# Longer iterations in the first convolution of a graph kernel: 12 gathered and 10 bucketed groups with 12 orderings, and an earlier load of the places

## The chip, the cores and the metric

The kernel runs on 1 core of one Trainium2 chip. The metric is the device time of one execution in microseconds (us), as the median of several runs; lower is better.

## The reference

The function works on a graph of 12500 nodes with 32 features each and 200000 edges, whose destinations are sorted and whose sources are random. It first applies a layer normalisation and an equivariant message-passing layer (a small network per edge, products with spherical harmonics, a sum over the edges at each destination). Then, after another normalisation, it applies three graph convolutions, of 32 to 128, 128 to 128 and 128 to 32 features:

```
h = x @ W
msg = h[src] * norm[:, None]
out = segment_sum(msg, dst) + b      # self loops are among the edges
```

with a rectifier after each. The change concerns only the first of the three convolutions (n = 1 in the code). There the kernel sums the rows of a normalised table (96 bf16 numbers per node: three bf16 parts of 32 features) over the edges, before it multiplies by W1.

## The kernel before

**Two ways to fetch a source's row.** In each convolution the edges are divided. "Gathered" groups of 1024 edges fetch the rows of their sources from DRAM: SyncE loads the 1024 indices (L556), GpSimd issues 8 indirect DMAs of 128 rows (L676), and TensorE sums the 8 tiles into a window of 128 destinations with a one-hot matrix (`gathered_sum`, L1860); VectorE adds the window to the accumulator `accT` (L1532) and makes the next group's one-hot matrix (L1434). Four row buffers rotate, so GpSimd may start group g only when group g-4 has been added. "Bucketed" groups of 1408 edges never touch the table in DRAM: their edges were ordered by the block of 128 nodes that holds the source, and one-hot matrices on both sides, made on the chip, pick and sum the rows of a table that lies in SBUF.

**Chunks.** A bucketed group is worked off in NCK = 5 chunks. For each chunk ScalarE makes the source matrix for the chunk that follows, in two instructions (`near_sources` L845, `mark_sources` L854), and copies out what TensorE took (`copy_bucket` L867); TensorE takes 20 small products (`take`, L1790) and gives 5 (`give`, L1804); VectorE makes the destination matrix (L1419). All these are double buffered, by chunk, with each wait on the chunk two before. The source matrices need the group's "places", an 800 KB load that spreads one row of DRAM over 128 partitions (`load_places`, L828, issued by ScalarE). It has two buffers, by the parity of the group.

**Ordering.** The places are themselves computed in the first convolution, for all 96 bucketed groups of the kernel: 2 before it starts, 94 during it. One ordering ("rank") takes three chunks: VectorE compares (`count_blocks`, L1322 first) when k % 3 is 0, TensorE counts (L1765), ScalarE copies the counts (`copy_prefix`, L836) when k % 3 is 1, VectorE ranks (`rank_edges`, L1337 to L1359), TensorE spreads (`place_values`, L1772 and L1774) and VectorE keeps the result (`keep_places`, L1365 to L1372) when k % 3 is 0 again, just ahead of the next `count_blocks`. ScalarE stores it to DRAM (`store_places`, L818) when k % 3 is 2. Of the ranks of an iteration the first OWN are for this convolution's own groups, the others for groups that only the later convolutions take.

**The loop.** `sweep` writes the first and the last iteration out, with constants, and runs those between in a hardware loop. `LOOP[n]` and `REST[n]` say how many gathered and bucketed groups an iteration and the last one have. Before the change they are (8, 6) and (12, 16) for n = 1: 10 iterations of 30 chunks with 8 ranks each (9 of them in the loop), and a last one of 80 chunks with 14 ranks. In an iteration the ranks fill chunks 0 to 23, and chunks 24 to 29 have none; in the last they fill chunks 0 to 41, and 42 to 79 have none. Gathered groups start at evenly spread chunks (`shape`).

**The load's place.** The load of the next group's places is issued in a group's third chunk (c == 2), after that chunk's `copy_bucket`, and after its `copy_prefix` if it has one. It waits until the store of those places has landed. The places are first read in the body of the group's last chunk (c == 4), where ScalarE runs `near_sources` for the next group's first chunk.

Of the kernel before, what the change touches and what calls it, by code (L numbers as in the profile page):

```python
# [38 lines left out]
UNROLL = 4  # L39
# [16 lines left out]


GATHERED = [NG, 92, 100, 64]
LOOP = [(UNROLL, 0), (8, 6), (12, 8), (8, 12)]
REST = [(UNROLL, 0), (12, 16), (16, 14), (8, 12)]  # L60
ITS = [NIT] + [(GATHERED[n] - REST[n][0]) // LOOP[n][0] + 1 for n in (1, 2, 3)]
E0 = GATHERED[3] * GE
BJ = 11
# [12 lines left out]
BIAS = F3  # L76
KC = 5

RANKS = 8
OWN = LOOP[1][1]  # L80
SLOTS = 2
RANKING = 13
NCK = KB // KC
# [8 lines left out]
OWN_LAST = BUCKETED[1] - 2 - OWN * (ITS[1] - 1)  # L92
RANKS_LAST = OWN_LAST + OTHERS - (RANKS - OWN) * (ITS[1] - 1)
assert RANKS % SLOTS == 0 and 3 * RANKS <= LOOP[1][1] * NCK and OWN_LAST == REST[1][1] - 2
assert OWN_LAST <= RANKS_LAST and 3 * RANKS_LAST < REST[1][1] * NCK


NORM0 = sqrt(4 * pi) / sqrt(2 * MUL)
# [21 lines left out]
def gnn_kernel(nc, x, src, dst, edge_attr, edge_weight, w1, b1, w2, b2,  # L120
               W1, B1, W2, B2, W3, B3, out):
    ctx = ExitStack()
    with ctx:
# [575 lines left out]
        def _(act):  # L699
# [170 lines left out]
            def conv(n):  # L870

                def body(step, first, last):
                    groups, chunks_, starts_at = shape(n, last)
                    u = -1
                    for k in range(chunks_):
                        if k in starts_at:
                            u, at = u + 1, k
                            held = (starts_at + [chunks_])[u + 1] - k
                            ahead = n == 2 and not (last and u == groups - 1)
                        more = not (last and k == chunks_ - 1)  # L880
                        if n == 1 and more:
                            near_sources(step, k + 1)
                        if ahead and k == at:
                            onehot_waits(n, step, u + 1, first)
                            distances(step, u + 1, range(TPG // 2))
                        if ahead and k == min(at + 1, at + held - 1):
                            distances(step, u + 1, range(TPG // 2, TPG)).then_inc(dist_ready[(u + 1) % 2], 1)
                        if ahead and k == min(at + 2, at + held - 1):
                            onehot_of_distances(n, step, u + 1)
                        if n == 1 and more:  # L890
                            mark_sources(step, k + 1)
                        copy_bucket(n, step, k)
                        v, c = divmod(k, NCK)
                        if n == 1 and k % 3 == 1 and k // 3 < (RANKS_LAST if last else RANKS):
                            copy_prefix(step, k // 3)
                        i = (k - 2) // 3 - 1
                        if n == 1 and k % 3 == 2 and 0 <= i < (RANKS_LAST if last else RANKS):
                            store_places(step, i, last)
                        if n == 1 and c == 2 and not (last and k + NCK >= chunks_):
                            load_places(n, step, v + 1)  # L900
                        if n > 1 and c == NCK - 1 and not (last and k + 2 * NCK >= chunks_):
                            load_places(n, step, v + 2)

                if n == 1:
                    near_sources(Step(act, 0, n), 0)
                    mark_sources(Step(act, 0, n), 0)
                if n == 2:
                    make_onehot(n, Step(act, 0, n), 0, True)
                sweep(act, body, n)

            def first_places(n):
# [46 lines left out]
        def _(dve):  # L958
# [538 lines left out]
            def conv(n):  # L1497
                rows_ = WIDTH[n]

                def ranking(step, k, last):  # L1500

                    i, part = divmod(k, 3)
                    most = RANKS_LAST if last else RANKS
                    if part == 0:
                        if 0 < i <= most:
                            keep_places(step, i - 1, last)
                        if i < most:
                            count_blocks(step, i, last)
                    elif part == 1 and i < most:
                        rank_edges(step, i, last)  # L1510

                def body(step, first, last):
                    groups, chunks_, starts_at = shape(n, last)
                    u = -1
                    for k in range(chunks_):
                        more = not (last and k == chunks_ - 1)
                        if more and n > 1:
                            mark_sources(n, step, k + 1)
                        mark_destinations(n, step, k)
                        if k in starts_at:  # L1520
                            u += 1
                            if u % UNROLL == 0:
                                start = load_registers(starts, step, u, N - 1)
                                n_far = load_registers(further, step, u, NB)
                            far_windows(n, step, u, n_far[u % UNROLL])
                            dve.wait_ge(*when(group_summed, step, u, before=convs_before(n)))
                            dve.wait_ge(*when(added, step, u - 1, before=rounds_before(n)))
                            v_done = (k - 7) // NCK
                            if not no_chunk(n, step, v_done * NCK):
                                dve.wait_ge(bucket_added, bucket_count(n, step, v_done))  # L1530
                            window = bass.ds(start[u % UNROLL], WIN)
                            v.tensor_tensor(accT[0:rows_, window], accT[0:rows_, window], sums[0:rows_, u % 2, 0:WIN],  # L1532
                                            ALU.add).then_inc(added[u % UNROLL], 1)
                            if n != 2:
                                if not (last and u == groups - 1):
                                    make_onehot(n, step, u + 1, first)
                                if not (last and u >= groups - 2):
                                    pair_numbers(n, step, u + 2)
                        if k % NCK == 1 and not (first and k == 1):
                            add_bucket(n, step, (k - 1) // NCK - 1, u)  # L1540
                        if n != 2 and k % NCK == NCK - 2 and not (last and k + 2 >= chunks_):
                            pair_destinations(n, step, k // NCK + 1)
                        if n == 1:
                            ranking(step, k, last)
                    if last:
                        add_bucket(n, step, chunks_ // NCK - 1, groups - 1)
                if n == 1:
                    dve.reg_mov(far_count, 0)
                if n != 2:
                    begin = Step(dve, 0, n)  # L1550
                    v.tensor_copy(iota_ps.bitcast(fp32), iota_h[:, :].bitcast(fp32))
                    v.tensor_copy(iota1_ps.bitcast(fp32), iota1_h[:, :].bitcast(fp32)).then_inc(iota_set, 1)
                    for u in range(2):
                        pair_numbers(n, begin, u)
                    pair_destinations(n, begin, 0)
                    dve.wait_ge(iota_set, 1 if n == 1 else 2)
                    make_onehot(n, begin, 0, True)
                if n > 1:
                    mark_sources(n, Step(dve, 0, n), 0)
                sweep(dve, body, n)  # L1560
                dve.wait_ge(bucket_added, sum(BUCKETED[:n + 1]))
                if n == 1:
                    v.tensor_reduce(odd_i[:, NBG:NBG + 1], odd_i[:, 0:NBG], X, ALU.max).then_inc(odd_counted, 1)
                    dve.wait_ge(odd_counted, 1)
                odd_edges(n)
                v.memset(flag[:, :], 0.0).then_inc(conv_done, 1)
# [63 lines left out]
        def _(pe):  # L1630
# [219 lines left out]
            def conv(n):  # L1850
# [14 lines left out]
                def body(step, first, last):  # L1865
                    groups, chunks_, starts_at = shape(n, last)
# [17 lines left out]
                                    place_values(step, i)  # L1884
                    if last:
                        give(n, step, chunks_ - 1)
                if n == 1:
                    pe.reg_mov(far_count, 0)
                    pe.wait_ge(acc_set, NCH)
                    for i in (-2, -1):  # L1890
                        count_prefix(Step(pe, 0, 1), i)
                        place_values(Step(pe, 0, 1), i)
# [86 lines left out]
```

## Time and profile before

| | before |
|---|---|
| median of 3 runs | 5388.06 us (5382.95 to 5391.85) |
| the profiled execution | 5381.47 us, its span 5379.6 us |
| busy over the span | PE 85%, PEld 60%, DVE 74%, ACT 58%, POOL 66% |
| mean granted TensorE clock | 0.85 of full speed |

The profile is one execution, followed instruction by instruction. PE is TensorE's matmuls, PEld its weight loads, DVE VectorE, ACT ScalarE, POOL GpSimd, SP SyncE; a "q" behind the name is that engine's issue of DMAs. A line number is that of the kernel above. A bracket behind an instruction says how long its engine had been idle before it, and what released it. The first convolution's first VectorE rank of the swept part is at 2365 us, its last instruction on the accumulator at 3450 us: some 1090 us of 5380.

### The profile page before, as it was taken

How to read it: one execution, taken by the hardware profiler on the slowest of the kernel's cores; microseconds unless marked ns; L12 is line 12 of the kernel's file. 1: busy time of each engine (PE TensorE's matmuls, PEld its weight loads, DVE VectorE, ACT ScalarE, POOL GpSimd, SP SyncE). 2: the span in 40 equal slices, each digit the busy share in tenths (PEclk: the TensorE clock that was granted, in tenths of full speed). 3: DMA queues.
4: the chain of work that ended last, by engine and by line, in shares of the span. 5: the costliest groups of instructions: out<-in, count | busy, mean ns of one | idle time of the engine just before them, and what ended most of it. 6: DMA issues, size and time to landing. Idle time of an engine off the chain costs nothing. (4 is left out here: it accounts for less than half of the span.)

```text
span 5379.6 us, 146653 instructions
## 1 busy us (share of the span) xinstructions
PE 4570.9 (85%) x51651; PEld 3244.5 (60%) x51652; DVE 3990.6 (74%) x9508; ACT 3122.0 (58%) x6228; POOL 3551.7 (66%) x3635
## 2 busy tenths in 40 slices
PE   2999999999999999946666666699999999877777
PEld 1555555555555555534555455588888899655656
DVE  5999999999999999977777777344444444366665
ACT  2666666666666666457777777655555554344442
POOL 3777777777777777457777774177777774177774
PEclk9999999999999999955555555699999999577676
DMA  6111111111111111232222222333333332344443
GB/s 73 37 36 36 36 36 38 36 36 36 36 38 36 36 36 36 34 64 76 76 77 76 83 76 70 112 104 110 104 110 104 110 106 80 98 143 146 139 152 99
DMA packets 464109, 398.70 MB, mean 74 GB/s; under 512 B 252172, under 2 KB 437360, under 8 KB 462948
## 3 DMA queue, kind: packets, MB, share of 16 engines
q10 hardware_dynamic: 143252, 205.78, 11.1%
q0 software_dynamic: 115712, 109.02, 9.4%
q1 hardware_dynamic: 204496, 75.06, 6.6%
q8 instruction: 430, 7.05, 0.5%
q14 instruction: 219, 1.79, 0.1%
HBM read 374.23 MB, written 15.28 MB: 72 GB/s over the span
## 5 line engine op out<-in xcount | busy, mean ns | idle before, releaser
L676 POOL DMA_INDIRECT rows<-table,idx x3616 | 3536.0, 978 | 1768.8 <-issue 1097.2
L733 ACT ACTIVATE dist<-iota,rel 128x128 f32<-128x128 f32 x2368 | 735.3, 391 | 840.0 <-PE sums L1684 804.9
L1684 PE MATMUL sums<-scratch,onehot 128*128 128x393 f32 x3136 | 1122.2, 500 | 50.9 <-DVE scratch L1176 47.0
L1673 PE MATMUL radial<-w2n,shared 65*128 65x384 f32 x3136 | 1081.3, 488 | 98.4 <-ACT shared L756 98.4
L1790 PE MATMUL radial<-arena,shared 128*32 128x96 bf16 (+1 forms) x31200 | 917.9, 264 | 272.8 <-ACT shared L854 182.7
L1684 PEld LDWEIGHTS sums<-scratch,onehot 128*128 128x128 f32 x3136 | 579.6, 190 | 553.8 <-issue 97.0
L1790 PEld LDWEIGHTS radial<-arena,shared 128*32 128x32 bf16 (+1 forms) x31200 | 654.3, 114 | 401.7 <-ACT shared L854 192.2
L1673 PEld LDWEIGHTS radial<-w2n,shared 65*128 65x128 f32 x3136 | 581.4, 190 | 512.0 <-ACT shared L756 98.0
L1152 DVE TENSOR_TENSOR scratch<-radial,shared 128x768 f32<-128x768 f32 x784 | 737.6, 941 | 0.0
L867 ACT CAST scratch<-radial 128x480 bf16<-128x480 f32 x860 | 473.5, 551 | 402.7 <-PE radial L1790 387.3
L1804 PE MATMUL psT<-shared,scratch 128*96 128x96 bf16 (+1 forms) x3900 | 475.9, 271 | 108.1 <-DVE shared L1419 97.6
L1804 PE MATMUL psX<-shared,scratch 128*96 128x96 bf16 (+1 forms) x3900 | 473.6, 271 | 79.0 <-DVE shared L1419 74.4
L1144 DVE TENSOR_TENSOR scratch<-radial,shared 128x512 f32<-128x512 f32 x784 | 529.7, 676 | 8.3 <-PE radial L1673 3.0
L1390 DVE TENSOR_SCALAR shared<-scratch,line 128x640 bf16<-128x640 bf16 (+1 forms) x830 | 396.6, 478 | 164.4 <-PE radial L1790 95.4
L1804 PEld LDWEIGHTS psT<-shared,scratch 128*96 128x96 bf16 (+1 forms) x3900 | 392.9, 179 | 188.8 <-DVE shared L1419 85.8
L1804 PEld LDWEIGHTS psX<-shared,scratch 128*96 128x96 bf16 (+1 forms) x3900 | 396.5, 180 | 150.1 <-DVE shared L1419 83.5
L1162 DVE TENSOR_REDUCE scratch<-scratch 128x64 f32<-128x1024 f32 x392 | 471.2, 1202 | 0.0
L756 ACT ACTIVATE shared<-shared,b1c,w1c 64x1024 f32<-64x1024 f32 x196 | 439.4, 2242 | 0.4 <-DVE relX L1064 0.4
L1532 DVE TENSOR_TENSOR accT<-accT,sums 96x128 f32 (+1 forms) x256 | 73.0, 285 | 488.7 <-PE sums L1860 473.9
L1860 PE MATMUL sums<-onehot,rows 128*128 128x128 f32 (+1 forms) x2848 | 361.2, 289 | 83.5 <-DMA rows<-table,idx 72.7
L863 ACT COPY scratch<-radial 128x384 f32<-128x384 f32 x350 | 167.4, 478 | 440.8 <-PE radial L1790 419.9
L1419 DVE TENSOR_TENSOR shared<-radial,shared 128x480 bf16<-128x480 bf16 x860 | 338.4, 399 | 107.0 <-PE psX L1804 37.9
(180 smaller groups left out, 4709.0 us busy)
## 6 DMA issues: line engine op xcount, KB each, us to landing
scratch<-places_d ACTq DMA_DIRECT2D x242, 800.0 KB
rows<-table,idx POOLq DMA_INDIRECT x3616
shared<-in_edge_weight SPq DMA_DIRECT2D x195, 256.0 KB, 3.5
idx<-in_src SPq DMA_DIRECT2D x451, 4.0 KB
arena<-norm_d ACTq DMA_DIRECT2D x4, 1568.0 KB, 12.3
table<-arena SPq DMA_DIRECT2D x24, 256.0 KB, 2.4
table<-arena SPq DMA_DIRECT2D x2, 1176.0 KB, 10.6
table<-arena SPq DMA_DIRECT2D x24, 96.0 KB, 2.0
```

Source lines behind the costliest of these rows:

```text
L676: (pool.indirect_dma_start(rows_3[:, r, j, :] if n in (1, 3) else rows[:, r, j, 0:WIDTH[n]], None, tables[n], bass.IndirectOffsetOnAxis(ap ...
L733: ins = nc.scalar.activation(dist[:, j, :], iota[:, :], ACT.Abs, scale=-1.0, bias=rel[:, bass.ds(step.tile(u) + j, 1)])
L756: nc.scalar.activation(hidT[0:HID0, u % 2, 0:tiles, 0:used], ew_row[:, u % 2, 0:tiles * used].rearrange("c (p j) -> c j p", j=tiles), ACT. ...
L867: nc.scalar.copy(taken[n][:, h, :, :], radial[0][:, h, 0:KC * F3].rearrange("p (t f) -> p t f", f=F3)).then_inc(bucket_copied, 1)
L1144: prod = v.tensor_tensor(prodA[:, h, t:t + 2, :].rearrange("p t (m s) -> p t m s", s=16), R[:, :, 0:256].rearrange("p t (m s) -> p t m s", ...
L1152: last = v.tensor_tensor(msg[:, h, t:t + 2, 17:401].rearrange("p t (i u s) -> p t i (u s)", i=3, u=MUL), R[:, :, 256:384].unsqueeze(2).to_ ...
L1162: v.tensor_reduce(msg[:, h, :, 0:16], prodA[:, h, :, :].rearrange("p t (m s) -> p t m s", s=16), X, ALU.add).then_inc(scalars_ready[h], 1)
L1390: v.tensor_scalar(from_src[n][:, k % 2, :, :, :], places[v_ % 2][:, :, c * KC * CAP:(c + 1) * KC * CAP].rearrange("p i (t r) -> p i t r", ...
L1673: last = nc.tensor.matmul(radial[q % 2][:, k, 0:RDIM], hidT[:, u % 2, 2 * q + k, :], w2n[:, :], start=True, stop=True)
L1684: last = nc.tensor.matmul(sums[:, u % 2, 0:SEGW], onehot[:, u % 2, 4 * h + k, :], msg[:, h, k, MUL:MUL + SEGW], start=(h == 0 and k == 0), ...
L1790: last = nc.tensor.matmul(d, from_src[n][:, h, i, t, :], table_of(n, s), start=True, stop=True, tile_position=(0, 32 * i))
L1804: last = nc.tensor.matmul((psX if v % 2 else psT)[0:w, 0:BWIN], taken[n][:, h, t, :], to_dst[n][:, h, t, :], start=(c + t == 0), stop=(c * ...
```

## The change

The first convolution's iterations become longer: LOOP (12, 10) and REST (8, 6), with 12 ranks in each. ITS[1] falls from 11 to 8: 7 iterations of 50 chunks (6 of them in the loop) and a last one of 30. The groups of each kind stay 92 and 76, the ranks 94. In an iteration the ranks now fill chunks 0 to 35 and chunks 36 to 49 have none; the last iteration has 10 ranks, which fill all of its 30 chunks, and the end of the tenth is written out behind the chunks. The next group's places are loaded in a group's second chunk instead of its third.

```
-LOOP = [(UNROLL, 0), (8, 6), (12, 8), (8, 12)]
-REST = [(UNROLL, 0), (12, 16), (16, 14), (8, 12)]
+LOOP = [(UNROLL, 0), (12, 10), (12, 8), (8, 12)]
+REST = [(UNROLL, 0), (8, 6), (16, 14), (8, 12)]
...
-RANKS = 8
+RANKS = 12
...
-assert OWN_LAST <= RANKS_LAST and 3 * RANKS_LAST < REST[1][1] * NCK
+assert OWN_LAST <= RANKS_LAST and 3 * RANKS_LAST == REST[1][1] * NCK
...
-                        if n == 1 and c == 2 and not (last and k + NCK >= chunks_):
+                        if n == 1 and c == 1 and not (last and k + NCK >= chunks_):
                             load_places(n, step, v + 1)
...
+                    if last and n == 1:
+                        store_places(step, RANKS_LAST - 1, last)
...
+                    if last and n == 1:
+                        keep_places(step, RANKS_LAST - 1, last)
                     if last:
                         add_bucket(n, step, chunks_ // NCK - 1, groups - 1)
...
                     if last:
                         give(n, step, chunks_ - 1)
+                    if last and n == 1:
+                        place_values(step, RANKS_LAST - 1)
```

## Rows read from the trace of the kernel before

**Rows 1.** Busy time by stage: a looped iteration, then chunks of the last without ranks.
```profile
core 0: us, PE busy (x) PEld busy (x) DVE busy (x) ACT busy (x) POOL busy (x), PEclk, DMA share, GB/s
2542.30:2630.30 88.00, 54.95 (x989) 44.71 (x993) 64.55 (x224) 62.29 (x97) 62.86 (x65) 0.52 0.29 78
3363.50:3433.30 69.80, 39.04 (x800) 29.82 (x800) 19.84 (x67) 60.74 (x91) 12.35 (x14) 0.51 0.24 77
```
**Rows 2.** Waits in the first convolution, 2355.8 to 3450.2 us: total, times, longest.
```profile
ACT arena L836 <- PE radial L1765: 127.3, 73, 2.8
ACT shared L845 <- DMA scratch<-places_d: 125.6, 64, 9.8
POOL rows L676 <- DVE accT L1532: 111.6, 46, 11.8
...
DVE arena L1337 <- ACT arena L836: 32.8, 50, 2.7
```
**Rows 3.** L1322 on VectorE, one instruction for each rank: count, first and last start.
```profile
L1322 DVE TENSOR_TENSOR arena<-radial,arena x94: 871/892/893, 2365.0 to 3357.1; 128x1408 bf16<-128x1408 bf16 x94
```
**Rows 4.** Timeline of L1322 on VectorE: a looped iteration, and the last's first rank.
```profile
3068.80 0.88 DVE L1322 TENSOR_TENSOR arena<-radial,arena 128x1408 bf16<-128x1408 bf16 x1
...
3077.68 0.89 DVE L1322 TENSOR_TENSOR arena<-radial,arena 128x1408 bf16<-128x1408 bf16 x1
...
3086.67 0.89 DVE L1322 TENSOR_TENSOR arena<-radial,arena 128x1408 bf16<-128x1408 bf16 x1
...
3095.45 0.89 DVE L1322 TENSOR_TENSOR arena<-radial,arena 128x1408 bf16<-128x1408 bf16 x1
...
3132.12 0.89 DVE L1322 TENSOR_TENSOR arena<-radial,arena 128x1408 bf16<-128x1408 bf16 x1
...
3157.73 0.88 DVE L1322 TENSOR_TENSOR arena<-radial,arena 128x1408 bf16<-128x1408 bf16 x1
...
3244.55 0.88 DVE L1322 TENSOR_TENSOR arena<-radial,arena 128x1408 bf16<-128x1408 bf16 x1
```
**Rows 5.** Timeline of ScalarE after an iteration's last rank: loads, waits and free chunks.
```profile
3134.54 0.41 ACTq L828 DMA_DIRECT2D scratch<-places_d  x1
...
3138.75 0.83 ACT L845 ACTIVATE shared<-scratch,line 128x640 bf16<-128x640 bf16 x1 [1.62 <-DMA scratch<-places_d]
...
3140.78 0.83 ACT L845 ACTIVATE shared<-scratch,line 128x640 bf16<-128x640 bf16 x1
...
3145.91 0.41 ACTq L828 DMA_DIRECT2D scratch<-places_d  x1
...
3150.77 0.83 ACT L845 ACTIVATE shared<-scratch,line 128x640 bf16<-128x640 bf16 x1 [1.75 <-DMA scratch<-places_d]
```
**Rows 6.** Timeline at the loop's return: TensorE's last and next take; VectorE's first instruction.
```profile
3148.62 0.59 PE L1790 MATMUL radial<-arena,shared 128*32 128x96 bf16 x20 [0.87 <-ACT shared L854]
...
3151.56 0.41 DVE L1419 TENSOR_TENSOR shared<-radial,shared 128x480 bf16<-128x480 bf16 x1 [3.37 <-issue]
...
3154.56 0.59 PE L1790 MATMUL radial<-arena,shared 128*32 128x96 bf16 x20 [4.78 <-ACT shared L854]
```
**Rows 7.** Waits from 3360 to 3450 us, the last iteration's chunks without ranks.
```profile
ACT shared L845 <- DMA scratch<-places_d: 8.8, 7, 2.9
```
**Rows 8.** Timeline of VectorE: one rank from its first to its last instruction; the convolution's end.
```profile
2547.62 0.89 DVE L1322 TENSOR_TENSOR arena<-radial,arena 128x1408 bf16<-128x1408 bf16 x1
...
2556.43 0.18 DVE L1372 CAST shared<-arena 128x32 f32 x1
...
3449.94 0.25 DVE L1494 TENSOR_TENSOR accT<-accT,psX 96x96 f32 x1 [3.14 <-PE psX L1804]
```
**Rows 9.** Timeline of ScalarE: a store in chunk 5, `copy_bucket` of chunk 6, `copy_prefix` in 7.
```profile
2463.37 0.38 ACTq L818 DMA_DIRECT2D places_d<-src_at  x1
...
2465.93 0.54 ACT L867 CAST scratch<-radial 128x480 bf16<-128x480 f32 x1
...
2470.98 0.27 ACT L836 CAST arena<-radial 128x128 bf16<-128x128 f32 x1 [1.87 <-PE radial L1765]
```
**Rows 10.** Writes to DRAM: KB each, us from issue to landing.
```profile
table<-arena SPq DMA_DIRECT2D x24, 96.0 KB, 2.0
...
bucket_start_d<-arena SPq DMA_DIRECT2D x1, 0.4 KB, 7.3
```
**Rows 11.** Instruction fetches of the iteration from 2542.3 to 2630.3 us: packets, MB, share.
```profile
q8 instruction: 11, 0.18, 0.9%
```
**Rows 12.** GpSimd's gathers in the same iteration: busy, mean ns, idle before them.
```profile
L676 POOL DMA_INDIRECT rows<-table,idx x65 | 63.8, 981 | 25.4 <-issue 20.2 <-DVE accT L1532 5.3
```

## Prediction

> **What bounds the kernel now.** Only the first convolution changes, so I read that stretch, 2356 to 3450 us. The table by stages comes first [rows 1]: in a looped iteration of 88.0 us VectorE is busy 64.6, ScalarE 62.3 and GpSimd 62.9 us, so no engine is full; where no ranks run, ScalarE is busy 60.7 of 69.8 us, and it sets the pace. Then the waits [rows 2]: GpSimd waits 111.6 us for VectorE's adds. It is ahead of the others by its four buffers, so the gathers don't bound. ScalarE waits 127.3 us for a rank's counts and 125.6 us for places. The question is which of these waits lie on the path.
>
> The starts of L1322, one per rank, give the rhythm [rows 3, 4]. From the first to the eighth rank of an iteration it is 3132.12 - 3068.80 = 63.3 us, 9.05 per rank of three chunks. From the eighth to the next iteration's first it is 25.6 us, for nine chunks of which six have no rank. Ten iterations take 3244.55 - 2365.0 = 879.6 us, so the mean gap from a last rank to the next first is 87.96 - 7 x 9.05 = 24.6 us. The last iteration's 13 intervals take 3357.1 - 3244.55 = 112.6 us, and from its last rank to the final add it is 3450.2 - 3357.1 = 93.1 us [rows 3, 4, 8]. So the convolution is 83 intervals (633.5 + 112.6 = 746.1 us), ten gaps (246) and a tail (93.1): 1085 us.
>
> In a chunk without a rank ScalarE needs 3140.78 - 3138.75 = 2.03 us, unless it waits for places: 1.62 us in chunk 24 and 1.75 us in chunk 29 [rows 5]. Each return of the loop costs more: TensorE's take of the next iteration comes 3154.56 - 3148.62 = 5.94 us after the last one where 2.03 is the rhythm, 3.9 us lost, and VectorE had nothing to run for 3.37 us [rows 6]. The wait of chunk 29 lies inside this: the source matrix was ready at 3150.77 + 1.69 = 3152.5 us, TensorE began 2.1 us later. (The 1.69 is two instructions of 0.83 and the step between them.)
>
> **The change part by part.** Chunks (380), gathers, ranks (94) and ranks in written-out code (22) keep their numbers.
>
> *Intervals.* They grow from 83 to 86 (7 x 11 + 9): +3 x 9.05 = **+27.2 us**.
>
> *Gaps.* They fall from ten to seven, and each gets 8 more chunks without a rank at 2.03: 24.6 + 16.3 - 1.6 = 39.3 us. The 1.6 is chunk 24's wait for places, which the earlier load ends (below). 7 x 39.3 = 275 against 246: **+29 us**. Three returns of the loop less, 11.7 us, are in this.
>
> *Tail.* It had 38 chunks without a rank. Now the tenth rank ends the iteration: from L1322 to its last kept value a rank takes 2556.43 + 0.18 - 2547.62 = 9.0 us [rows 8]. TensorE's last give stands ahead of the values (0.6 us, the take of 20 being the nearest row of its size [rows 6]), and the value read and final add stand behind (I take 0.9, of which the add is 0.25): 10.5 us. 93.1 to 10.5: **-82.6 us**. Nothing hides these 10.5 us. The last store and the load for the second convolution come later by this much too; that load is covered by the tables made between the convolutions, and uncovered it would cost its landing, under 5 us.
>
> *The load one chunk earlier.* Its issue is followed by the landing after 3138.75 - 3134.54 = 4.2 and 3150.77 - 3145.91 = 4.9 us. ScalarE was free 1.75 us before the second landing, 3.1 us after the issue; one more chunk makes this 5.1 us, so the wait goes. In the gaps and the tail it is counted above. Among ranks ScalarE has slack: it waits for the counts anyway. There I compare two intervals with one gathered group each, the second (3077.68 to 3086.67, 8.99 us) with a wait for places and the third (8.78) without [rows 4]: 0.21 us per load, and three of five loads wait in this way, some 35 in all: **-7.4 us**. The bounds of this term are 0 (ScalarE's slack hides all) and the whole wait: 125.6, less 8.8 in the last iteration's tail [rows 2, 7] and about 10 x (1.6 + 1.75) in the gaps, is 83 us. I take the value near 0 because it is the one measured on intervals. At the seven returns that remain the load's wait is worth nothing, since TensorE is later; at most 7 x 1.75 = 12 us.
>
> *A store just ahead of a load.* The places of an iteration's third group are stored in chunk 5 and were loaded in chunk 7; now they are loaded in chunk 6, some 3.0 us behind the store (2463.37 to 2465.93 + 0.44) [rows 9]. No row shows when such a store has landed. The nearest writes to DRAM took 2.0 and 7.3 us [rows 10]. With 2.0 nothing waits. With 7.3 ScalarE waits 4.3 us with the next `near_sources` queued behind, of which 1.87 us were idle before the counts [rows 9]: 2.4 x 8 = +19 us. I take 0, since the 7.3 us was a write of 4 bytes per descriptor. The Trainium skill (DMA: Bandwidth & Descriptors, Anatomy of one DMA) puts a DMA's fixed cost at about 2.0 us and adds that a write to HBM can take surprisingly long; by its 2.0 the sum would be the same, by its warning nearer to +19.
>
> *Gathers.* A group costs GpSimd 8 x (0.98 + 0.31) = 10.3 us [rows 12], the 0.31 being 20.2 us of issue over 65. Twelve take 124 us of an iteration that I put at 11 x 9.05 + 39.3 = 139 us, so its lead stays.
>
> **Sum.** 27.2 + 29 - 82.6 - 7.4 = -34 us, from 5381.5 us of the profiled execution to 5347.5. This execution was 6.6 us below the median of the runs; from the median the forecast is **5354 us**. The layout alone would give little: with waits for places at 1.3 to 1.8 us left in the gaps (42.2 us each) it is 27.2 + 49.3 - 82.6 = -6 us. The load's place is most of the gain.
>
> **Rivals.** *The rank's chain runs through ScalarE's wait as well.* For it: ScalarE reads the counts right after it catches up, and VectorE waits 32.8 us for that copy [rows 2]. Against: the interval pair above. If half to all of the 83 us came back, 5388 - 34 - (34 to 76) = 5278 to 5320.
>
> *The wait for places stays.* The load lands later because it meets other transfers, or the gain is taken up by a later wait. For it: landings differ by 0.7 us between two neighbours and the longest wait is 9.8 us [rows 2, 5]. Against: the margin of 5.1 us covers both. It would leave the layout's -6: 5382.
>
> *The store is late*, as above: -34 + 19, 5373.
>
> *Slower: the longer body is not fetched in time.* An iteration fetches 11 packets of instructions for 30 chunks [rows 11], so the whole body is fetched anew each time; 50 chunks make 18, about 130 in seven iterations. The one place where a fetch shows is the loop's return, 3.4 us of idle VectorE [rows 6]. If one packet in five were waited for at that price, it is 26 x 3.4 = +88 us, and 5442; the sign turns at 10 packets (34 us). Against it: inside an iteration no engine shows such a stall now, over 10 x 11 packets. The Trainium skill (Runtime: NRT & Kernel Launch, Instruction fetch mechanics) says that the fetch of sequential blocks is mostly hidden and a taken branch out of the window stalls; by it this rival gives 0 and the three returns saved stand.
>
> **How the numbers follow.** Forecast 0.66, its own range 5335 to 5375; rank chain 0.13; waits stay 0.12; late store 0.04; slower 0.05. The range of 8 in 10 goes from 5308, inside the first rival, to 5383, past the second. What a measurement can tell from no change is about 0.2%, 10.8 us. Faster takes the forecast, the first rival and the late store, 0.83; within 0.2% the waits that stay, 0.12; slower 0.05.
>
> **What would show it.** Right: the wait of L845 for places falls from 125.6 to below 20 us; free chunks at 2.03 us throughout; L1322 intervals near 9.0 us, seven gaps near 39 us, and about 10 us from the last L1322 to the final add; GpSimd still waiting for L1532. Wrong: a gap above 42 us; a wait of ScalarE for a store of places in chunk 6; intervals of 8.5 us or less, which would mean the first rival; idle "issue" time of TensorE or VectorE inside an iteration, which would mean the last.

## The result, and the profile after

The kernel after takes **5365.11 us** (median of 5 runs, 5359.89 to 5372.49), the kernel before on the same chip 5387.14 us (5 runs, 5379.18 to 5391.85). The ratio is 0.9962, with an interval of 0.9951 to 0.9973: about 20 us faster. The profiled execution of the kernel after took 5365.11 us with a span of 5363.1; the one of before took 5381.5 us, with a span of 5379.6. So the two traces differ by 16.5 us, less than the medians do.

The forecast was 5354 us, inside a range of 5308 to 5383. The total falls in it, but that hides two things which nearly undo each other: the first convolution gained as much as was forecast, and the second, which the change doesn't touch, lost half of it again. The rows that show it are the end marks of the convolutions, a MEMSET of `flag` at the end of each. In the kernel before:

```profile
3451.40 0.06 DVE L1566 MEMSET flag<- 128x1 f32 x1 [0.93 <-DVE odd_i L1563]
...
4579.80 0.06 DVE L1566 MEMSET flag<- 128x1 f32 x1 [0.91 <-DVE accT L1494]
...
5333.30 0.06 DVE L1566 MEMSET flag<- 128x1 f32 x1 [1.25 <-issue]
```

In the kernel after, the same timeline of VectorE:

```profile
3417.31 0.06 DVE L1570 MEMSET flag<- 128x1 f32 x1 [1.24 <-issue]
...
4562.74 0.06 DVE L1570 MEMSET flag<- 128x1 f32 x1 [0.92 <-DVE accT L1496]
...
5316.86 0.06 DVE L1570 MEMSET flag<- 128x1 f32 x1 [0.91 <-DVE accT L1496]
```

The first convolution ends 3451.40 - 3417.31 = 34.1 us sooner. The second takes 4562.74 - 3417.31 = 1145.4 us where it took 1128.4: **17.0 us more**. The third takes 754.1 against 753.5. The sum, -34.1 + 17.0 + 0.6 = -16.5, is the difference of the spans.

**The first convolution after.** L1324 is the rank's first instruction, which was L1322. Its count and its first and last start (to [rows 3]), then the table by stages for one looped iteration (to [rows 1]):

```profile
L1324 DVE TENSOR_TENSOR arena<-radial,arena x94: 872/891/892, 2365.1 to 3406.4; 128x1408 bf16<-128x1408 bf16 x94
```

```profile
core 0: us, PE busy (x) PEld busy (x) DVE busy (x) ACT busy (x) POOL busy (x), PEclk, DMA share, GB/s
2774.42:2913.44 139.02, 90.02 (x1641) 72.49 (x1644) 101.04 (x348) 104.91 (x163) 94.82 (x96) 0.52 0.32 80
```

An iteration of 50 chunks takes 139.02 us, as the prediction put it (139). The shares are near those of [rows 1]: VectorE 0.73 in both, ScalarE 0.75 against 0.71, GpSimd 0.68 against 0.71. The timeline of L1324 shows where an iteration's ranks end and the next one's begin (to [rows 4]):

```profile
2774.42 0.88 DVE L1324 TENSOR_TENSOR arena<-radial,arena 128x1408 bf16<-128x1408 bf16 x1
...
2873.15 0.89 DVE L1324 TENSOR_TENSOR arena<-radial,arena 128x1408 bf16<-128x1408 bf16 x1
...
2913.44 0.88 DVE L1324 TENSOR_TENSOR arena<-radial,arena 128x1408 bf16<-128x1408 bf16 x1
```

From the first to the twelfth rank it is 98.73 us, 8.98 per interval, and the gap to the next iteration is 40.3 us. The waits of the first convolution, 2355.8 to 3417 us (total, times, longest; to [rows 2]):

```profile
ACT arena L836 <- PE radial L1769: 173.8, 94, 2.7
...
POOL rows L676 <- DVE accT L1534: 102.4, 44, 4.3
...
ACT shared L845 <- DMA scratch<-places_d: 15.1, 13, 9.6
```

ScalarE's wait for places fell from 125.6 to 15.1 us, and its wait for a rank's counts rose from 127.3 to 173.8. That is the slack among ranks: ScalarE comes earlier to a wait that was there before. A store in chunk 5 and the load that depends on it in chunk 6, on ScalarE (to [rows 9]):

```profile
2786.82 0.37 ACTq L818 DMA_DIRECT2D places_d<-src_at  x1
...
2787.78 0.83 ACT L845 ACTIVATE shared<-scratch,line 128x640 bf16<-128x640 bf16 x1
2788.85 0.38 ACTq L828 DMA_DIRECT2D scratch<-places_d  x1
...
2789.82 0.83 ACT L845 ACTIVATE shared<-scratch,line 128x640 bf16<-128x640 bf16 x1
```

The load goes out 2.03 us behind the store, and the next L845 comes 2.04 us after the last: nothing waited. At the loop's return (the jump back to the start of its body) the first instruction of TensorE and of ScalarE in the next iteration (to [rows 6]):

```profile
2910.26 0.59 PE L1794 MATMUL radial<-arena,shared 128*32 128x96 bf16 x20 [3.44 <-issue]
...
2910.24 0.83 ACT L845 ACTIVATE shared<-scratch,line 128x640 bf16<-128x640 bf16 x1 [2.16 <-issue]
```

And the end, from the last rank's kept value to the final add (to [rows 8]); the last L1324 starts at 3406.4:

```profile
3414.75 0.16 DVE L1374 CAST shared<-arena 128x32 uint8<-128x32 f32 x1
3415.55 0.25 DVE L1496 TENSOR_TENSOR accT<-accT,psX 96x96 f32 x1 [0.64 <-issue]
```

The tail is 3417.31 - 3406.4 = 10.9 us to the mark, where before it was 94.3 to the mark.

**The second convolution after.** TensorE is its bound: from 3417 to 4562 us it is busy 1113.78 of 1145 us. The rows list each fp32 product of the kernel as two matmuls, so the 20 products of a take are x40. TensorE's timeline at returns of this convolution's loop:

```profile
3839.18 0.73 PE L1794 MATMUL radial<-arena,shared 128*32 128x128 f32 x17 [2.02 <-DVE shared L1392]
3842.97 1.51 PE L1794 MATMUL radial<-arena,shared 128*32 128x128 f32 x23 [3.07 <-issue]
...
4098.38 0.73 PE L1794 MATMUL radial<-arena,shared 128*32 128x128 f32 x17 [2.42 <-issue]
4101.69 1.50 PE L1794 MATMUL radial<-arena,shared 128*32 128x128 f32 x23 [2.58 <-issue]
```

The take of 40 matmuls is cut after the 17th, and TensorE stands still with nothing that the profile shows it to wait for. The convolution has eight iterations, of which the first and the last are written out and six are run by the loop, so the loop returns five times. All five returns show this cut, with idle times of 1.70, 3.07, 2.79, 2.58 and 2.58 us; the step into the loop and the step out of it show none. The kernel before has one gap at a return, ahead of the take, and none inside or behind it:

```profile
4122.72 2.26 PE L1790 MATMUL radial<-arena,shared 128*32 128x128 f32 x40 [2.40 <-issue]
4124.91 2.69 PE L1860 MATMUL sums<-onehot,rows 128*128 128x128 f32 x16
```

The table by windows says the same. Before, then after, one stretch of 250 us of the second convolution (TensorE's busy time is the first number behind the length):

```profile
3750.00:4000.00 250.00, 245.41 (x4376) 221.26 (x4376) 109.23 (x200) 142.20 (x376) 189.98 (x198) 0.99 0.35 108
```

```profile
3750.00:4000.00 250.00, 240.02 (x4245) 216.22 (x4240) 106.10 (x194) 136.58 (x361) 189.02 (x197) 0.97 0.36 104
```

5.4 us of 250 are lost here, with two returns in it; VectorE and ScalarE do less in the same time because they wait for TensorE.

The gaps are not all of the loss. Over the second convolution TensorE is idle for 31.6 us where it was 18.9, 12.8 more, and busy for 1113.8 us where it was 1109.6, 4.2 more for the same 19394 matmuls. The clock has a part in this. Ten us from the start of the first take behind a return, before and then after:

```profile
4122.72:4132.72 10.00, 10.00 (x159) 9.03 (x160) 3.69 (x8) 5.11 (x14) 7.71 (x8) 0.83 0.28 77
```

```profile
4098.38:4108.38 10.00, 7.42 (x90) 6.58 (x94) 0.94 (x3) 3.19 (x10) 4.06 (x5) 0.66 0.23 61
```

A granted clock of 0.83 is 3.4 us of the 10 at the 1.2 GHz level, and 0.66 is 6.8 us. It comes behind the idle time at the return. In the kernel before it is 3.4 us long at four of the five returns and absent at one; in the kernel after it is 6.8 us at all five, and so it is in the four other versions with the loss. The 16 matmuls behind the take then need 3.61 us at this return, where the kernel before needs 2.69. So the clock adds to what the gaps cost.

**The theories.** What has to be settled is which part of the change gained the 34 us, and what lost the 17. For the loss, theory A: the new loop body shifted TensorE's instruction stream behind it, so that the target of the second loop's return now lies just ahead of the boundary of a block that is fetched as one, and the block behind it comes too late. An iteration's fetches support a block of this kind, 16.4 KB per packet:

```profile
q8 instruction: 16, 0.26, 0.8%
```

Theory B: something else that the layout leaves behind when the second convolution starts (the late last store, the load behind it, the state of the buffers). Theory C: the load's place.

### The profile page after: what moved, and what is told of

Read it like the earlier page. It is cut to its first block, busy times and chain, and to the rows that moved or that the text cites. A ratio compares the mean times of both kernels' runs of the same rounds, so it can differ in the third digit from the quotient of the medians.

```text
span 5363.1 us, 146734 instructions
## 1 busy us (share of the span) xinstructions
PE 4561.7 (85%) x51651; PEld 3237.4 (60%) x51652; DVE 3982.0 (74%) x9508; ACT 3120.8 (58%) x6228; POOL 3548.8 (66%) x3635
## 4 chain that ended last, share of the span: by engine, by line
PE 27%; POOL 9%; issue 8%; DVE 8%; ACT 2%; DVEq 1%; DMA 1%; ACTq 0%; POOLq 0%; SPq 0%
POOL rows L676 9%; PE radial L1794 8%; PE psT L1808 5%; PE psX L1808 4%; PE sums L1864 4%; PE radial L1769 2%; ACT shared L845 1%; DVE arena L1324 1%; DVE arena L1347 1%; PE radial L1925 1%; DVE arena L1343 1%; PE radial L1961 1%; PE radial L1776 1%; PE sums L1933 1%; ACT scratch L867 1%
## 5 line engine op out<-in xcount | busy, mean ns | idle before, releaser
L1864 PEld LDWEIGHTS sums<-onehot,rows 128*128 128x128 f32 (+1 forms) x2848 | 318.5, 190 | 133.5 <-DMA rows<-table,idx 69.6
```

The lines of the kernel that those rows point to most:

```text
L1864: mm = nc.tensor.matmul(sums[0:w, u % 2, 0:WIN], far_rows[j], (onehot if n == 2 else onehot_3)[0:used, u % 2, j, :], start=(j == 0), stop= ...
```

## Experiments

**One part alone.** The first kernel is after with the load back at a group's third chunk, the second is before with the load at the second.

```diff
-                        if n == 1 and c == 1 and not (last and k + NCK >= chunks_):
+                        if n == 1 and c == 2 and not (last and k + NCK >= chunks_):
```

> The changed kernel with the load of the places back in a group's third chunk. From the prediction: in the first convolution -6 us against before (that is 28 us more than the changed kernel has), with L845 waiting some 100 us or more for places again. Theory A (the 17 us that the second convolution lost come from where its loop lies in TensorE's instruction stream): this kernel's stream on TensorE is that of the changed one, so the second convolution takes 1145 us as in the changed kernel, and the whole is -6 + 17 = +11 us against before. Theory B (they come from the earlier load or from what it moves in DRAM): the second convolution is back at 1128 us and the whole is -6.

Measured: 5402.93 us against 5385.64, ratio 1.0037 (1.0024 to 1.0051): **slower than before**, by 17 us where +11 was expected. Its first convolution ends at 3454.47 us, 3.1 behind before, and ScalarE waits 130.9 us for places. Its second takes 1148.6 us and has the same cut:

```profile
4138.48 0.73 PE L1794 MATMUL radial<-arena,shared 128*32 128x128 f32 x17 [2.65 <-issue]
4142.06 1.51 PE L1794 MATMUL radial<-arena,shared 128*32 128x128 f32 x23 [2.85 <-issue]
```

```diff
-                        if n == 1 and c == 2 and not (last and k + NCK >= chunks_):
+                        if n == 1 and c == 1 and not (last and k + NCK >= chunks_):
```

> The kernel before with the load of the places one chunk earlier and nothing else. From the prediction's terms: 16 us of waits in chunk 24 of ten iterations, 9 us in the last iteration's chunks without ranks, 7 us among the ranks: -32 us in the first convolution (range -25 to -60). Theory A: TensorE's stream is that of before, so the second convolution stays at 1128 us and the whole is -32 us. Theory B: the second convolution loses up to 17 us here, and the whole is -15.

Measured: 5340.58 us, ratio 0.9915 (0.9902 to 0.9929): some 25 us better than the whole change. That is 45 us faster than the kernel before, where 32 was expected. The first convolution ends at 3415.92 us in a profile that took 5346.2 us, 5.6 above this median: 35.5 sooner than in before. The second takes 1127.2. So the load's place is the gain, and the loss comes with the layout: theory C falls. On the first convolution the layout brought nothing: +3.1 us with the late load, and 3417.31 - 3415.92 = +1.4 with the early one, both within the scatter of single profiles (below).

**The stream shifted, the layout kept.** Both kernels put unneeded matmuls ahead of the second convolution in TensorE's stream: 16 in the kernel after, 30 in the kernel before. What they do is move everything that follows in the stream.

```diff
                 if n == 2:
+                    for i in range(16):
+                        nc.tensor.matmul(psT[0:1, 500:501], one[:, :], one[:, :], start=True, stop=True)
                     pe.wait_ge(acc_set, 2 * NCH)
```

> The changed kernel with 16 tiny matmuls (64 instructions of TensorE) between the first and the second convolution, in an unused corner of a PSUM bank. Theory A: the target of the second convolution's loop no longer lies some 36 instructions ahead of a 16 KB boundary, nor the third's some 14 ahead; the second gap inside the first take (17 of 40 matmuls, 2.6 to 3.1 us idle, 23 more) goes from every return; the second convolution falls from 1145 to about 1128 us, and the whole to -33 us against before. Theory B (data, buffers or the other engines' streams): the second convolution stays at 1145 us or gains under 4 us.

Measured: 5351.94 us, ratio 0.9936 (0.9923 to 0.995). More work, and 13 us faster than the kernel after. The cut is gone, the second convolution takes 1127.4 us, and TensorE is as busy as in before:

```profile
3750.00:4000.00 250.00, 245.06 (x4336) 221.40 (x4337) 107.84 (x199) 140.54 (x374) 190.29 (x197) 0.99 0.37 108
```

> The kernel before with 30 tiny matmuls (120 instructions of TensorE) at the same place, which puts both later loops at the place in the stream that they have in the changed kernel, within one instruction. Nothing else changes. Theory A: the second convolution rises from 1128 to about 1145 us with the take of 40 split 17 and 23 at each return, and the whole is +17 us against before. Theory B: no change beyond 3 us for the 30 matmuls.

Measured: 5405.93 us, ratio 1.0035 (1.0022 to 1.0049), the second convolution 1146.5 us. The old layout with the old load has the loss too once the stream behind it is shifted, and the cut now falls after the 13th matmul, where the 17th was expected:

```profile
4007.63 0.63 PE L1790 MATMUL radial<-arena,shared 128*32 128x128 f32 x13 [2.10 <-DVE shared L1390]
4010.93 1.92 PE L1790 MATMUL radial<-arena,shared 128*32 128x128 f32 x27 [2.67 <-issue]
```

Theory B falls with these two: the same layout with and without the loss, and the loss without the layout. The ten profiles at a mean granted clock of 0.85, those of the runs below included, fall into two groups in the second convolution: 1127.2 to 1128.8 us where no take is cut or followed by a gap, 1144.1 to 1148.6 where one is.

**How the loss grows with the place.** A first attempt: the same edit with 16 and 24 matmuls in the kernel before, and in a third kernel each group's places loaded yet a chunk earlier:

> The kernel before with 16 tiny matmuls (64 instructions of TensorE) at the same place as in the other padded kernels. The second convolution's loop target then lies about 93 instructions ahead of a 16 KB boundary of TensorE's stream (157 in the kernel before, 36 in the changed one), the third's about 70. Theory A (a second fetch is waited for only as far as the instructions between the target and the boundary don't cover it, about 0.02 to 0.03 us each in a take of fp32): the second gap is shorter by 57 instructions than in the changed kernel, 1 to 2 us instead of 2.8, and the second convolution takes 1132 to 1140 us. If the padding itself cost anything, it would show here as well: under 2 us. Rival (any crossing near the target costs the whole 17 us): 1145 us.

> The same with 24 tiny matmuls (96 instructions): the target about 61 instructions ahead of the boundary. Theory A: a gap between that of the 64-instruction kernel and the changed kernel's, 1138 to 1144 us in the second convolution. Rival: 1145 us, or 1128 where only very few instructions ahead of the boundary hurt.

```diff
-                        if n == 1 and c == 2 and not (last and k + NCK >= chunks_):
+                        if n == 1 and c == (1 if v == 1 else 0) and not (last and k + NCK >= chunks_):
```

> The kernel before with the places loaded in a group's first chunk (in the second group of an iteration in its second chunk, because that group's places are stored in its first). Against the kernel with the load alone in the second chunk, which waited 19.6 us for places of which 9.9 us once at the start: the remaining waits go, of which most lie where TensorE is later anyway. -35 to -42 us in the first convolution against before, 0 to -5 against that kernel; if ScalarE instead waits for the store of the same group's places (stored one to two chunks earlier), up to 3 us per iteration come back and it is slower than that kernel.

Measured: 8076.35, 8097.0 and 8064.88 us, with ratios of 1.0006 (0.9985 to 1.0027), 1.0021 (1.0002 to 1.004) and 0.9991 (0.9971 to 1.0011). On this chip every kernel took about 8,070 us at that time, before too (8072.4), with a mean granted clock of 0.73 where the other profiles have 0.85. Effects of a few microseconds don't stand out there, and the three answer nothing. They were run again:

> The kernel before with 16 unneeded matmuls (64 instructions of TensorE's stream) between the first and the second convolution. Stream-place theory with a graded cost: the second convolution's return target now lies some 93 instructions ahead of a 16 KB boundary (157 before, 36 in the kernel after), and TensorE crosses it only after the second packet has come, so the second convolution takes 1128 to 1140 us against 1128.4 before. Theory that any 16 added matmuls cost it something of the size seen with 30: 1137 us or more. The first convolution is unchanged in either case (flag at 3451 us).

Measured: 5404.06 us, ratio 1.0035 (1.0021 to 1.0048), the second convolution 1144.1 us. This is the whole loss, where theory A as I had put it, with a cost that grows with the place, allowed 1140 at most. The size was missed; the place was not. The gap now stands between the take of 40 and the next take of 16:

```profile
4008.62 1.68 PE L1790 MATMUL radial<-arena,shared 128*32 128x128 f32 x40 [2.98 <-issue]
4012.57 3.77 PE L1860 MATMUL sums<-onehot,rows 128*128 128x128 f32 x16 [2.27 <-issue]
```

> The same with 24 unneeded matmuls (96 instructions): the target lies some 61 instructions ahead of the boundary. Stream-place theory: the first take of 40 matmuls after a return is cut or nearly cut, and the second convolution takes 1136 to 1146 us, between the kernel before (1128.4) and 30 such matmuls (1146.5). A theory in which the place does nothing and only their number counts: 64 and 96 instructions lie on a line from 0 to the +18 us of 120, so +9.6 and +14.4 us.

Measured: 5401.04 us, ratio 1.0031 (1.0019 to 1.0043), the second convolution 1147.8 us, 1.8 above my range. The count theory wanted +9.6 and +14.4 us for the two, and they have +15.7 and +19.4, with +18.1 for 30 matmuls: no line through zero. The cut is after the 25th:

```profile
4006.65 0.95 PE L1790 MATMUL radial<-arena,shared 128*32 128x128 f32 x25 [2.37 <-issue]
4009.95 1.08 PE L1790 MATMUL radial<-arena,shared 128*32 128x128 f32 x15 [2.36 <-issue]
```

From 30 to 24 unneeded matmuls the cut moves from 13 to 25, two matmuls of the take for each one taken out. With eight fewer again it should be at 25 + 16 = 41, just behind the take of 40, which is where the kernel with 16 has it. For the kernel after, 16 unneeded ones move the cut from 17 to -15, that is, ahead of the target, and no return meets it. One rule fits these places. It isn't known why 30 unneeded matmuls, which were to put the loop where it stands in the kernel after, put the cut four matmuls sooner (13 for 17). The gap at the cut is 1.2 to 3.2 us over the 25 returns of the five kernels. The boundary itself is in no view; what the traces show is that the gap moves with the length of the stream, by the length added.

That leaves the question why the kernel before, whose boundary lies some 73 matmuls of this kind behind the target, doesn't pay. From the start of the first take to the first matmul behind the cut it is 3842.97 - 3839.18 = 3.8 us in the kernel after, 3.3 with 24 and 30, and 3.95 with 16 in the rows above, and 3.0 to 3.95 over all 25 returns, whatever stands ahead of the cut. So it looks like a race: TensorE can go past the boundary 3.0 to 4.0 us after the return has been served, and it loses what it reaches the boundary too early by. The trace's packets of queue q8 agree. At each of the 50 returns of the ten profiles one packet starts 0.4 to 1.3 us behind the start of the take and is done 1.5 to 2.3 us behind it, with or without a loss; where there is a cut, TensorE goes on 1.2 to 1.8 us after the packet. The trace doesn't say which engine a packet is for. A kernel between 0 and 16 tests this:

> The kernel before with 8 unneeded matmuls (32 instructions): the second convolution's return target lies some 125 instructions ahead of the boundary, between the kernel before (157, no second gap) and 16 such matmuls (93, a second gap and 1144 us). If TensorE and the fetch race each other, TensorE reaches the boundary about 1.3 us (40 matmuls) and two thirds of the next take of 16 (2 to 3.8 us) after the return, which is about the 3.3 to 4.0 us that the next packet took, so the gap is under 1 us and the second convolution takes 1128 to 1134 us. If what counts is only that unneeded matmuls stand there, it takes 1140 us or more, as with 16, 24 and 30.

Measured: 5390.22 us, ratio 1.0007 (0.9998 to 1.0016), the second convolution 1128.8 us, and no gap behind the take:

```profile
4003.32 2.36 PE L1790 MATMUL radial<-arena,shared 128*32 128x128 f32 x40 [3.71 <-issue]
4005.61 3.77 PE L1860 MATMUL sums<-onehot,rows 128*128 128x128 f32 x16
```

By the same rule the boundary is 25 + 32 = 57 of the take's matmuls behind the target: 40 are the take, the 16 behind it have the same two instructions each in the trace (one load of weights, one matmul), and a few waits stand between. That puts it at the end of the 16. The quickest of the five returns shows it there:

```profile
4256.77 1.30 PE L1790 MATMUL radial<-arena,shared 128*32 128x128 f32 x40 [2.32 <-DVE shared L1390]
4258.04 1.94 PE L1860 MATMUL sums<-onehot,rows 128*128 128x128 f32 x15
4260.23 0.38 PE L1860 MATMUL sums<-onehot,rows 128*128 128x128 f32 x1 [0.26 <-issue]
```

TensorE comes to the 16th 3.2 us after the take's start, stands for 0.26 us and goes on at 3.5, inside the 3.0 to 4.0 of the other kernels. At the other four returns it comes there after 4.4 us or more, and there is no gap. Eight more unneeded matmuls bring the boundary to 1.3 to 2.4 us after the start (the take's own length), and the second convolution loses 15 us. So the forecast of the race came true, and the theory that unneeded matmuls cost something by being there falls.

**The load one chunk earlier still.**

> The kernel before with each group's places loaded at its first chunk (the group that opens the body at its second). If what is left of the gain of the earlier load is lead, the first convolution ends 0 to 5 us sooner than with the load at the second chunk (flag at 3411 to 3416 us, against 3415.9 there and 3451.4 before) and the wait for places falls below the 19.6 us in all that it had there. If the second chunk is early enough, flag and wait stay as there, and the run gives 5338 to 5346 us.

Measured: 5340.81 us, ratio 0.992 (0.9906 to 0.9933), the first convolution's end at 3411.80 us, 4.1 sooner than with the load at the second chunk. The wait for places is one single wait:

```profile
ACT shared L845 <- DMA scratch<-places_d: 9.9, 1, 9.9
```

The total is the same as with the load at the second chunk (0.9915). The 4.1 us are below what a measurement tells and within the scatter of single profiles, so a further gain isn't shown. These two, the old layout with an earlier load, are the best versions found, and both beat the kernel after and the kernel before.

## Why the prediction was right, and the step that was wrong

**The total** was right for reasons that were partly its own, partly luck: an undersized gain and an unforeseen loss.

**The first convolution, term by term.** Intervals are counted between starts of the rank's first instruction inside iterations, gaps between the last rank of one and the first of the next. All numbers are changes against the profile of before, in us.

| term | forecast | measured |
|---|---|---|
| intervals (86 for 83) with the early load | +27.2 - 7.4 = +19.8 | 762.4 - 744.4 = +18.0 |
| gaps (7 for 10) | +29 | 278.9 - 247.7 = +31.2 |
| tail, to the mark | -82.6 | 10.95 - 94.3 = -83.3 |
| sum | -34 | -34.1 |
| layout alone | -6 | +3.1 |
| load in the new layout | -28 | -37.2 |

The gap came out at 39.8 us on average where 39.3 was forecast, and 43.7 with the late load (42.2 forecast); that 1.5 us, seven times, is the layout's missing gain. The load's gain in the new layout splits into -27.3 in gaps (forecast 7 x 2.9 = -20) and -9.8 among ranks (-7.4). Among ranks in the old layout it was 4.3 us. So the term taken near zero, by one pair of intervals, was the right end of its range: of the 110.5 us less that ScalarE waited for places, 46.5 came back as waiting for counts.

The prediction treats every gap as one with a return and speaks of seven returns that remain. The loop holds nine iterations before and six after, so there are eight returns and five. Three fewer is right, but in the kernel before the gaps with a return are 25.1 us on average and the two without are 23.6, so a return lengthened a gap by 1.5 us and not by the 3.9 read from one timeline. The wait for places hid the rest: with the load alone moved, the two kinds are 23.3 and 19.7 us, and in the kernel after 40.8 and 37.6. So it was right that chunk 29's wait is worth nothing at a return (1.8 us gained there, about chunk 24's wait), and at the two gaps without one it was worth as much again (3.9 us gained).

The sizes of the parts rest on single profiles, and these scatter. Five programs have the code of before up to the end of the first convolution (before, and 8, 16, 24 and 30 unneeded matmuls behind it), and their marks are at 3451.4, 3458.8, 3457.7, 3452.9 and 3455.4 us; the profile of before is the lowest. Against their mean of 3455.2, the whole change is worth -38 us there, the layout alone -1, the early load alone -39. This also closes the books with the medians: -38 + 17 is -21, and 22.0 was measured. The forecast of -34 was thus some 4 us small, and the load's share more so: 28 was forecast, and the load alone gained 39 us by its profile and 45 by the medians.

**The rivals.** That the rank's chain runs through ScalarE's wait is answered by the interval pair having been right: 8.91 us per rank inside the seven iterations after, 9.03 inside the ten before, not 8.5. The waits for places did not stay (15.1 us). The late store did not come: the load went out 2.03 us behind the store with no idle time, so the 8 KB had landed by then. The prediction set the Trainium skill's 2.0 us (DMA: Bandwidth & Descriptors, Anatomy of one DMA) beside its warning about writes to HBM. That section is on DMAs that GpSimd issues, and this store is issued by ScalarE; the trace agrees with the 2.0 in so far as the write took at most 2.03 us.

**The step that failed is the first sentence's: "Only the first convolution changes".** Its rival on the slower side had named the right resource, the fetch of instructions, and the wrong place. It looked for stalls inside the longer body; the only ones over 1 us on TensorE, VectorE and ScalarE are at the return, where they were before (in the kernel after ScalarE 2.16 us, TensorE 3.44 in the rows above), and the sum came out without a term for more of them. The loss came at the returns of the *next* loop, whose body didn't change by one instruction. Its five returns cost 17.0 / 5 = 3.4 us more each: 2.5 us of the second gap (12.7 us in all), and most of the rest from the longer stretch at the 1.2 GHz level. The Trainium skill (Runtime: NRT & Kernel Launch, Instruction fetch mechanics) says that instructions come in blocks of 256, fetched in order, and that a taken branch out of the window stalls. The trace agrees on the stall and on the block (16.4 KB per packet), but my use of that rule, "it gives 0", was too generous: only the block with the target is waited for by it, while the traces show a second wait, which by its place is for the block behind, if the target stands close ahead of a boundary. The prediction took it that the untouched convolutions keep their time, and this term, put at nothing, measured +17 us.

**Where the same gap costs nothing.** The third convolution's loop also has a cut take at each of its five returns in the kernel after, 2.5 to 3.0 us of idle time each:

```profile
4838.97 0.50 PE L1794 MATMUL radial<-arena,shared 128*32 128x96 bf16 x14 [2.74 <-issue]
```

Yet that convolution takes 754.1 us against 753.5, and 750.4 to 757.5 over the ten profiles. TensorE is busy 573 of its 755 us there, and 1114 of 1145 in the second. A stall of an engine that has slack is absorbed, and one of the engine that is the bound is paid in full.

**Left open.** The boundary and the engine that a packet is for are in no record; that the gap is a wait for the next block is argued from its place and from the packets' times. Open too is why 30 unneeded matmuls put the cut at 13 and not at 17. Not tried was the combination of the new layout, the shifted stream and the load at the first chunk: with the stream shifted, the new layout already stands 11 us behind the old one (0.9936 against 0.9915), with intervals that just overlap, so nothing spoke for it.

## What to carry to other kernels

Test the parts of a change alone even when their sum is faster: here the move of one load by one chunk was the whole gain, and the rebuilt loop around it cost it half. After any change of a loop's body, read the later loops as well, at their returns: a take cut in two by "issue" time on the engine that is the bound is worth more than its few microseconds, because it comes back at each return, and a few unneeded instructions ahead of the loop can remove it, or bring it. When spans are summed, compare several executions of the unchanged part first; here they scattered by 7 us.

## What the runs showed of the hardware

A return of a loop can stall an engine twice. The first gap, ahead of the first instruction, is 1.9 to 3.7 us on TensorE at the returns of the second convolution, in every version. The second appears with 13, 17, 25 and 40 matmuls of the take between the loop's target and the place of the cut. With the place at the end of the 16 behind the take it shrinks to 0.26 us at one return of five, and farther behind the target there is none. It is 1.2 to 3.2 us long, and TensorE goes on 3.0 to 4.0 us after the first instruction has started, wherever the boundary is. The loss went from nothing (8 unneeded matmuls, 1128.8 us) to its whole size (16 of them, 1144.1 us) in one step of eight unneeded matmuls.

A lower clock goes with the gaps. At all 25 returns with the second gap a stretch of 6.8 us at the 1.2 GHz level follows the idle time. At the 25 others of the ten profiles this stretch is 3.4 us long, with three exceptions: twice there is none, and once it is 6.8 us, behind the longest first gap (3.71 us). At the 1.2 GHz level the 16 matmuls behind the take start 0.21 us apart, at the 2.4 GHz level 0.11 us.
